# Three wide products of zeros ahead of everything on TensorE, fewer small ones there, in a fused retention and feed-forward layer

## The reference: what is computed

```
xn = _layernorm(x, axis=-1)
x = x + _L0_attn_ref(xn, rel_pos, Wq, Wk, Wv, Wo) + _L0_ffn_ref(xn, fast_b, w_fc, w_proj, u, v, gate)
```

```
h = _bitlinear(x, w_fc) + gate * (x @ v.T @ fast_b.T @ u.T)
r = jnp.maximum(h, 0.0)
return _bitlinear(r * r, w_proj)
```

## Time and profile before

| | |
|---|---|
| median of 3 runs | 126.28 us |
| all runs | 125.96, 126.28, 126.89 us |
| the profiled execution | 125.74 us |
| its span, first to last instruction | 123.8 us |
| PE busy | 117.4 us (95%) |
| DVE, ACT, POOL busy | 86.0, 85.3, 67.3 us |

### The profile page before, as it was taken

One profiled execution on the slowest core, in us unless ns is written; L12 is line 12 of the kernel. 1 busy time (PEld: TensorE's weight loads), 2 busy tenths in 40 slices (PEclk: granted clock), 3 DMA queues, 4 the chain that ended last, 5 costly groups with the idle time before them and its releaser, 6 DMA issues.

```text
span 123.8 us, 6395 instructions
## 1 busy us (share of the span) xinstructions
PE 117.4 (95%) x2876; PEld 92.3 (75%) x2876; DVE 86.0 (69%) x241; ACT 85.3 (69%) x166; POOL 67.3 (54%) x64
## 2 busy tenths in 40 slices
PE   4979999999999999999999999999999999998891
PEld 2427966778897778787887788788877787886680
DVE  0587997989794988767994988497958247521632
ACT  3455959799686966589659938686859755894410
POOL 7079933999729540963276524944295409655000
PEclk9999999999999999999999999999999999999999
DMA  3767748600000000000006000200010000200022
GB/s 93 233 239 184 324 87 339 265 0 8 5 0 5 0 5 5 0 0 0 0 0 254 3 0 0 85 0 0 0 69 18 0 0 0 90 5 5 5 85 85
DMA packets 2783, 7.73 MB, mean 62 GB/s; under 512 B 320, under 2 KB 832, under 8 KB 2512
## 3 DMA queue, kind: packets, MB, share of 16 engines
q1 hardware_dynamic: 2304, 7.05, 16.4%
q10 hardware_dynamic: 464, 0.47, 1.1%
HBM read 5.42 MB, written 2.10 MB: 61 GB/s over the span
## 4 chain that ended last, share of the span: by engine, by line
PE 91%; DVE 3%; ACT 2%; issue 1%; POOL 1%; DVEq 0%; POOLq 0%
PE ps_work L723 10%; PE ps_out L824 8%; PE ps_work L724 8%; PE ps_work L727 8%; PE ps_score L792 7%; PE ps_score L861 6%; PE ps_out L836 5%; PE ps_score L862 5%; PE ps_out L805 4%; PE ps_score L774 3%; PE ps_score L775 3%; PE ps_score L776 3%; PE ps_score L739 3%; PE ps_score L874 2%; PE ps_score L880 2%; PE ps_score L865 1%
## 5 line engine op out<-in xcount | busy, mean ns | idle before, releaser
L338 POOL TENSOR_TENSOR sq_lo<-square,sq_hi 128x512 fp32r<-128x512 f32 x31 | 39.4, 1286 | 16.0 <-ACT sq_hi L406 16.0
L583 DVE TENSOR_TENSOR scores<-ps_score,cst 128x512 f32<-128x512 f32 x32 | 20.0, 683 | 10.8 <-PE ps_score L792 10.8
L343 POOL TENSOR_TENSOR q_pair<-q_dec,cst 128x1024 f32<-128x1024 f32 x7 | 13.3, 1895 | 20.8 <-DVE q_dec L567 20.8
L397 ACT ACTIVATE square<-ps_work 128x512 f32<-128x512 f32 x30 | 17.5, 596 | 9.3 <-PE ps_work L727 7.0
L406 ACT ACTIVATE sq_hi<-square 128x512 fp32r<-128x512 f32 x32 | 20.1, 631 | 0.8
L402 ACT ACTIVATE square<-square 128x512 f32<-128x512 f32 x32 | 19.9, 622 | 0.0
L723 PE MATMUL ps_work<-xn_hi,w_hi 128*128 128x512 f32 x28 | 11.8, 422 | 0.0
L608 DVE TENSOR_TENSOR o_lo<-ps_out,o_hi 128x512 fp32r<-128x512 f32 x7 | 4.8, 692 | 10.0 <-ACT o_hi L415 9.9
L861 PE MATMUL ps_score<-sq_hi,w 128*128 128x512 f32 x28 | 11.7, 417 | 0.0
L824 PEld LDWEIGHTS ps_out<-scores,v_pad 64*32 64x32 f32 x896 | 9.3, 105 | 2.6 <-issue 2.6
L724 PE MATMUL ps_work<-xn_hi,w_lo 128*128 128x512 f32 x28 | 11.1, 396 | 0.0
(11 more groups left out here) (147 smaller groups left out, 259.0 us busy)
## 6 DMA issues: line engine op xcount, KB each, us to landing
resid<-x_feat SPq DMA_DIRECT2D x1, 2048.0 KB, 8.4
out_feat<-resid SPq DMA_DIRECT2D x7, 256.0 KB, 2.2
x_in<-x_tok SPq DMA_DIRECT2D x1, 1280.0 KB, 6.5
x_in<-x_tok SPq DMA_DIRECT2D x3, 256.0 KB, 3.7
po_in<-ffn_weights SPq DMA_DIRECT2D x1, 320.0 KB, 3.0
fc_in<-ffn_weights SPq DMA_DIRECT2D x1, 256.0 KB, 4.3
q_table<-q_decay SPq DMA_DIRECT2D x1, 256.0 KB, 3.3
wqvk<-qvk_weights ACTq DMA_DIRECT2D x1, 192.0 KB, 4.3
```

The source lines that it names most:

```text
L338: nc.gpsimd.tensor_tensor(sq_lo[p][:, f, :], square[p][:, f, :], sq_hi[p][:, f, :].bitcast(F32), ALU.subtract).then_inc(lo_ready, 1)
L397: nc.scalar.activation(square[b.parity][:, f, :], hidden_bank(b, f)[:], ACT.Relu).then_inc(relu_ready, 1)
L583: nc.vector.tensor_tensor(scores[b.parity][:, g].rearrange("p t s i -> p (t s) i"), ps_score[:, g].rearrange("p (a i) -> p a i", i=BLK), c ...
```

## The change

PE starts with three wide products of zeros in place of eight small ones and one wide. Six small ones are added behind the product with `u`, and those behind the transposes are thirteen in place of ten. The ten between the two products of the low-rank term stay. In all there are 29 small products (28 before) and three wide ones (one before): three products of four instructions more, so that the rest of PE's program stands 12 places further on. No other engine's program changes.

```
             zeros = v_pad[0][:, 0:2].rearrange("p t g c -> p (t g c)")
             pe.wait_ge(zeroed, 1)
-            place_program(8, ps_score[:, 0], zeros)
-            zero_products(1)
+            zero_products(3)
             pe.wait_ge(rank_loaded, 16)
             mm(ps_w1[0:RANK, 0:D], fb_in, v_in, start=True, stop=True).then_inc(fbv_done, 1)
             place_program(10, ps_score[:, 0], zeros)
             pe.wait_ge(fbv_gated, 1)
             mm(ps_w1, fbv[:], u_in, start=True, stop=True)
+            place_program(6, ps_score[:, 0], zeros)
             pe.wait_ge(consts_in, 16)
             turn_xn(first)
-            place_program(10, ps_score[:, 0], zeros)
+            place_program(13, ps_score[:, 0], zeros)
             pe.wait_ge(wqvk_split, 1)
             project_q(first)
             project_k(first)
```

## The result

| | before | after |
|---|---|---|
| median | 126.41 us (4 runs, 125.96 to 126.89) | 128.93 us (4 runs, 128.35 to 129.93) |
| the profiled execution | 125.74 us | 129.93 us |
| its span | 123.8 us | 128.1 us |

The ratio is 1.0207, 95% interval 1.0127 to 1.0287: the change is slower, by 1.3 to 2.9%. Two further comparisons gave 1.0175 (1.0111 to 1.0238) and 1.0142 (1.0095 to 1.0189). Forecast were 127.1 us and 0.6%, with 128.6 as the upper end. So the traces tell where time went, and the medians how much it is as a rule.

What follows compares the result with a forecast made beforehand. PE was taken as the bound (busy 117.4 us, 95%), with a chain of waits at the front. +2.24 - 0.2 - 0.2 - 0.5 = +1.3 us on the profiled 125.74 gave 127.1 us; range 125.8 to 128.6.

Steps and rivals of the forecast that it cites:

- The delay: At the front, the longer wide zeros make the product of `fast_b` and `v` 2.24 us later.
- k: How many of the six wide zero instructions pass at the lower clock level, 1.01 us each against 0.43; taken as 4.
- what comes back if the level stays up: Front work after the zeros runs at the upper clock level, winning back 0.2, 0.2 and 0.5 us.
- Term (a): Line 895's pair with the small products between, up to ACT's start: faster at the upper level, gains about 0.2 us.
- Term (b): Transposes: paced by DVE's tiles, but the last one is shorter at the upper level, gains 0.2 us.
- Term (c): Projections: line 727 starts earlier and the q and k matmuls run faster, gains 0.5 us.
- The first rival: Front: the clock level rises but does not last, or rises only after the zeros; 128.0 to 129.3 us, chance 0.18.
- the pause shrinks: Before the transposes: line 897 takes 0.9 us at the upper level and six small products follow, so PE waits less.
- The three small products behind the transposes: Extra small products there: hidden by ACT at the upper level, 0.23 us on the chain at the lower.
- The third rival: Whole program: the 12-place shift moves or adds PE stops, 0.45 us either way; 126.6 to 128.0 us, chance 0.06.
- The second rival: Initial zeros: the level rises almost at once, k at most 1; faster, 124.7 to 125.4 us, chance 0.08.
- The fourth: Behind the first batch: slack takes up the delay, so it does not reach the end; 125.5 to 126.9 us, chance 0.06.

Runs made afterwards that it cites:

- the one with the early table: The change plus one early square root on ACT, so the root's table loads before the wait for the low-rank product: 126.28 us, ratio 0.9993.
- the bridge: The change with two wide products of zeros and four small ones replacing the six small ones behind the product with `u`: 127.92 us, ratio 1.0088.
- the second trace shown above: Another profiled execution of the unmodified change, of the kind with mean granted clock 0.985 to 0.987: 129.28 us.
- it without the places: The change with ten small products behind the transposes instead of thirteen, so the later program is not shifted 12 places: 128.47 and 129.36 us, ratios 1.0129 and 1.0208.

## Why the prediction was wrong

**The delay was right.** k = 4.3 was measured for 4 (3.6 to 5.0 in six other traces with three wide products, and 2.9 in the one with the early table); `fbv` came 2.22 us later, forecast were 2.24 less 0.2. In the bridge, where the level stays up, the first score product starts 1.25 us later than before (16.05 against 14.80 in order of time), and the forecast's sum was 1.3. By ratio it is 0.9% slower.

**The step that failed is "what comes back if the level stays up".** It was given 0.62 of the chance and three terms, 0.2, 0.2 and 0.5 us. The level did not stay. In all sixteen runs of the change the mean clock was below 0.99. Term (a) came: the product and its small ones took 0.35 us from 6.82 to ACT, not 0.57. Term (b) was near nothing: the transposes took 1.15 us for 1.24. Term (c) had the wrong sign: from the start of line 723 to that of the scores it took 5.72 us (12.66 to 18.38), and before 4.64 (10.23 in the earlier trace rows to 14.87). That is 1.1 us lost in place of 0.5 won, because the second rise, at 16.5, came later relative to the projections than the only rise before, at 11.8. With 0.2 for the three small products this gives the 3.51 us: 2.31 - 0.09 + 0.21 + 1.08. In the other kind of execution, the second trace shown above, (c) is about nothing: 4.51 us (13.04 to 17.55, in order of time) for 4.57 before. And where the level does stay, in the bridge, the same stretch takes 4.07 (11.98 to 16.05): the 0.5 of term (c) was sized right, and its condition failed. The forecast asked only whether the projections run fast or as before; that they could run slower than before, with line 908 slow too, was in no rival.

**The first rival named the mechanism**, the pause in front of the transposes, with 128.0 to 129.3 us, and 128.93 lies there. It had 0.18 of the chance. It had (b) and (c) as nothing, so it too had no term for slower projections or for new stops, and it added its sum to a profiled execution that was 0.54 us below the median. So that the number lies within is in part luck. For it spoke a row that the prediction showed itself, 2.2 us in which line 739's weights waited before the only rise. That row was misread as time in which PE stood still: line 898's matmuls ran until 7.55 (5.48 + 2.07 in the earlier trace rows), and PE itself was idle for 0.66 us. The 1.47 us of PE's pause in the change are longer than the 0.66 before, where the prediction argued that the pause shrinks: line 897 at the upper level takes half the time, so it ends sooner and leaves more idle time, not less. That argument was turned the wrong way round. How far the pause itself is the cause: filling it took the fall out of the trace of the bridge and kept the mean clock at 0.996 or more in all its eleven runs, which is the evidence. But the fall does not always lie in it. In five traces, three of the change and two of it without the places, the level fell at 9.7, 10.2, 11.0, 10.2 and 12.2 us, the last 2.2 us after the pause had ended, amid the projections and 0.3 us after a second pause, of 0.32 us. The transposes are not the culprit: in the profiled execution the level was gone before they began. The Trainium skill, TensorE: Matmul & The Clock Gate, section Part 4: PE-mode transpose, says that the upper level doesn't engage for transposes. The trace does not agree: in the kernel with forty small zeros and the level up they take 328 ns and not 457, and the level survives them.

**The three small products behind the transposes** were to be hidden at the upper level and to cost 0.2 at the lower; the level was the lower, and the 26 instructions took 0.99 us for 0.78: 0.21, as priced for that case.

**The third rival** (places) was right that the stops belong to places and that 12 places leave the two at the end; it comes on top with an estimated 0.8 us, behind the front, and not as the main cause. The stops vary in length: 0.83 us in all before, 1.38 in the profiled execution of the change, 1.48 in one stop of another kernel. **The second rival** (an almost immediate rise) fell with k = 4.3. **The fourth** (slack) fell: nothing behind the front gave back any of the 3.51 us.

**The base.** The 127.1 us were the profiled execution's 125.74 and 1.3. Added to the median of 126.28 the same sum is 127.6, still below what was measured.

## What to carry to other kernels

Work that is put first to raise the clock is worth nothing if it delays an operand that another engine waits for, and the level it wins must be held: ask what PE does between the rise and the first real work, and remember that at the upper level the filler ends sooner and the pause grows. Price a lost level by what the work behind it then costs, not by what it would have won. Look at the other engine first: the chain went through a table load on ACT, and one instruction that loads it early was worth about 1.2%, more than any arrangement of zeros without it. And compare several traces of one kernel: here the level's first rise alone moved the front by more than a microsecond.

## What the runs showed of the hardware

The level can fall while PE is busy: in the kernel with two wide products and the early table it fell near 8.1 us, with PE busy 1.89 of the 2 us before, in small products, a product of 16 rows and transposes. Yet forty small products and an idle 0.6 us did not lower it in another. So neither idle time alone nor the width of the work alone decides here, and what does is open.

The page can hide the level: in the profile of before it grants 1.0 from the start, though the matmuls of the first 11.8 us ran at half speed by their durations (1.01 us for a wide one, 0.43 at the upper level); only where the level fell again did a page show a 5. So a mean granted clock of 1.0 doesn't say when the level first rose.

PE stops at places of the program, as the section on the twelve places shows. The stretch between the two stops at the end of the kernel before, from its trace (PE, then PEld, then the others):

```profile
112.45:116.33 3.88, 3.42 (x127) 2.71 (x128) 2.18 (x4) 2.08 (x4) 0.61 (x1) 1.00 0.02 4
```

127 matmuls and 128 weight loads lie between them, and so they do in the change:

```profile
116.70:120.60 3.90, 3.43 (x127) 2.72 (x128) 2.08 (x4) 1.99 (x4) 0.27 (x1) 1.00 0.02 4
```

255 instructions and, if there is one that isn't counted as busy, 256. Between the second and the third stop of the kernel before with 12 places more it is 128 and 128:

```profile
118.41:122.16 3.75, 3.75 (x128) 3.04 (x128) 1.47 (x3) 0.81 (x2) 0.00 (x0) 1.00 0.11 42
```

If one of the 11 loads of 16 KB holds 256 instructions, that is 64 bytes each. The Trainium skill, Runtime: NRT & Kernel Launch, section Instruction fetch mechanics, says that program is loaded in blocks of 256 instructions and that crossing one is mostly hidden; the distance agrees with the block. If the stops are waits for these loads, the hiding fails here, by 0.2 to 1.5 us a stop, amid dense small matmuls. That they are is an inference from the distance and from the places, not tested by itself; most places at that distance show no stop.
